# Planning of the counting: 16-bit operands, four buffers, short lists by way of memory, first projections ahead of the picks

## The chip, the core and the metric

The kernel runs on one core of a Trainium2 chip. The metric is the device time of one execution in microseconds. A core has TensorE (matrix products, with a clock that is granted at 1.2 or 2.4 GHz; "cold" and "warm" below), VectorE, ScalarE, GpSimd and SyncE, which here issues the DMAs. Each engine runs its own list of instructions; they meet at semaphores.

## The reference

A chain of four graph networks over 6250 nodes and 100000 edges, sorted by destination. What the step at hand prepares is the first one and the counting of edges for the later ones:

```python
Q = (h @ Wq.T).reshape(N, 8, 16); K = (h @ Wk.T).reshape(N, 8, 16); V = (h @ Wv.T).reshape(N, 8, 16)
score = einsum('ehd,ehd->eh', K[src], Q[dst]) / 4
s = exp(clip(score, -5, 5))[:, :, None]
wV = segment_sum(V[src] * s, dst); z = segment_sum(s, dst)
h_attn = (wV / (z + 1e-6)).reshape(N, 128)
...
agg = segment_sum(x[src], dst)     # in the later networks; here by a matrix of counts
```

## The kernel before, in words

Nodes are handled in 49 blocks of 128 (BLOCKS), in 7 groups (GROUPS) of 7 blocks (GB). Edges lie in tiles of 128; their tile numbers are kept in ROWS = 7 rows of 128 (COLS = 896 in all). For the later networks the kernel builds a matrix of counts in memory (`adjacency`), window by window: a window is 8 destination nodes, and a list of WCOLS = 1664 steps says which edge tile is counted into which window. The function `plan_windows` (L1895 to L2063) makes that list and what goes with it, between the first planning (`plan`) and the attention (`attend`), which starts when all engines have left it.

VectorE in `plan_windows`: after the iota and a memset of the ring of slots by GpSimd (L1943, L1944) and the load of `dst` and `src` (L1914) it casts both (L1960), makes `rank` (L1961 to L1963), copies the ramp four times over as 16-bit numbers (`fours`, L1964), and makes seven masks 1664 wide (L1968). TensorE multiplies each by ones (four products of 416 columns, L2048), which counts how many tiles begin by each step. VectorE reads the sums (`wtile`, L1970) and makes seven masks that pick the tile of each step (L1974). TensorE uses them to draw the rows of `dst` and `src` (eight products for each mask, L2054). Two buffers, `two`, carry the masks, in 32-bit numbers. VectorE makes `window` (L1975), waits for the picks, turns them into `ct.lo` and `ct.place` (L1978 to L1992), and then makes four lists of integers (`ct.tables`, L1996 to L2041), all on whole 128 x 1664 tiles of which it keeps 32 partitions each. `attend` and `score` read one partition of each list into registers.

TensorE's projections (Q, K and V of all blocks, one product of 384 columns for each block, L2062) wait for `taken`, which VectorE raises after it has read the picks (L1980). ScalarE copies each block out of PSUM (L1938, L1939) into `q` and into one of two staging buffers. SyncE loads `xT` for two groups ahead (L1919) and stores each group's K and V to the table in memory (L1928). From the third group on, ScalarE waits for the store of two groups earlier.

## Time and profile before

| | us |
|---|---|
| runs | 5399.48, 5402.13, 5411.69 (median 5402.13) |
| the profiled execution | 5400.67, span 5398.3 |
| `plan` | up to about 38.5 |
| `plan_windows` | 38.5 to 186.0 |
| granted TensorE clock over the span | 0.885 of full |

The page shows TensorE busy for 81% of the whole span, VectorE 66%, GpSimd 51% and ScalarE 42%; these are means over very different steps. For the step at hand one reads the stretches by engine first, and then the order in time of each engine.

### The profile page before, as it was taken

The numbers are of one execution on the slowest core, as the hardware profiler recorded it, in microseconds if no ns is written. First come the engines' busy times: TensorE is split into PE (matmuls) and PEld (weight loads), VectorE is DVE, ScalarE is ACT, GpSimd is POOL, SyncE is SP. The second block draws the span as 40 slices with busy tenths as digits, with TensorE's granted clock in tenths as the row PEclk, the third lists the DMA queues.
The fourth block names the chain that finished last, engine by engine and source line by source line (L and its number), as shares of the span: only waits on it lengthen the run. The fifth ranks groups of instructions, "written<-read, shape, count | busy, mean of one in ns | idle before, by whom it ended". The sixth has DMA issues, their size and how long they took to land. (4 is left out here: it accounts for less than half of the span.)

```text
span 5398.3 us, 99723 instructions
## 1 busy us (share of the span) xinstructions
PE 4350.4 (81%) x24072; PEld 3655.1 (68%) x24073; DVE 3580.8 (66%) x7929; ACT 2266.3 (42%) x4134; POOL 2766.0 (51%) x2730
## 2 busy tenths in 40 slices
PE   7566666766767777777468849999999999999998
PEld 4455555554344444444257639999999999999998
DVE  4888888888778888888776674444445654444444
ACT  0333434343245555555246644444444443344333
POOL 0477777774077777777221104444444443344433
PEclk8788888888977787777789959999999999999999
DMA  1444444443267777777235434343444443233332
GB/s 41 124 117 117 118 117 117 116 118 99 96 182 198 200 200 197 203 201 202 70 111 157 136 114 152 132 154 145 149 155 156 174 141 118 96 144 138 133 126 95
DMA packets 543103, 750.01 MB, mean 139 GB/s; under 512 B 57967, under 2 KB 441966, under 8 KB 542734
## 3 DMA queue, kind: packets, MB, share of 16 engines
q1 hardware_dynamic: 461182, 521.35, 28.8%
q0 software_dynamic: 81552, 224.63, 15.5%
q8 instruction: 123, 2.02, 0.1%
q14 instruction: 246, 2.02, 0.1%
HBM read 584.36 MB, written 161.41 MB: 138 GB/s over the span
## 5 line engine op out<-in xcount | busy, mean ns | idle before, releaser
L544 POOL DMA_INDIRECT arena<-table_kv,arena x1664 | 1721.9, 1035 | 653.5 <-issue 506.4
L2350 PE MATMUL ps<-moving,parts 128*128 128x384 f32 (+1 forms) x11662 | 2015.3, 331 | 36.3 <-ACT moving L2412 20.4
L2350 PEld LDWEIGHTS ps<-moving,parts 128*128 128x128 f32 x11662 | 1948.7, 188 | 70.1 <-ACT moving L2412 29.4
L2291 POOL CAST moving<-counts 128x1152 fp32r<-128x1152 uint8 (+1 forms) x420 | 476.7, 1135 | 736.8 <-PE ps L2350 604.7
L340 ACT ACTIVATE counted<-ps 128x392 uint8<-128x392 f32 x1568 | 665.0, 502 | 324.5 <-PE ps L331 283.7
L2291 POOL CAST moving<-big 128x1152 fp32r<-128x1152 uint8 (+1 forms) x413 | 468.4, 1134 | 608.6 <-PE ps L2350 608.6
L331 PE MATMUL ps<-by_place,by_lo 128*128 128x392 bf16 x1568 | 631.3, 525 | 101.9 <-DVE by_place L295 95.5
L654 PE MATMUL ps<-arena 128*128 128x137 f32 x1664 | 325.2, 352 | 338.1 <-DVE arena L788 322.3
L2412 ACT ACTIVATE moving<-counts 128x1152 fp32r<-128x1152 uint8 (+1 forms) x360 | 366.9, 1024 | 436.5 <-PE ps L2350 433.6
L2412 ACT ACTIVATE moving<-big 128x1152 fp32r<-128x1152 uint8 (+1 forms) x354 | 360.4, 1023 | 429.2 <-PE ps L2350 429.0
L654 PEld LDWEIGHTS ps<-arena 128*128 128x128 f32 x1664 | 276.8, 242 | 367.6 <-ACT arena L699 217.6
L2557 DVE CAST moving<-counts 128x1152 fp32r<-128x1152 uint8 (+1 forms) x240 | 312.8, 1303 | 287.2 <-PE ps L2350 287.2
L2557 DVE CAST moving<-big 128x1152 fp32r<-128x1152 uint8 (+1 forms) x236 | 307.5, 1303 | 288.8 <-PE ps L2350 288.8
L562 PEld LDWEIGHTS ps<-arena 128*128 128x128 bf16 x1680 | 141.6, 123 | 523.5 <-DVE arena L556 450.8
L321 DVE TENSOR_TENSOR slots<-slots,counted 128x196 uint16 x1568 | 406.6, 259 | 89.1 <-DVE slots L321 43.0
L562 PE MATMUL ps<-arena 128*128 128x128 bf16 x1680 | 199.6, 252 | 271.5 <-DVE arena L556 269.0
L295 DVE TENSOR_TENSOR by_place<-count_fours,count_place 128x1568 bf16<-128x1568 f16 (+1 forms) x497 | 395.6, 796 | 0.0
L331 PEld LDWEIGHTS ps<-by_place,by_lo 128*128 128x128 bf16 x1568 | 187.7, 123 | 249.2 <-issue 179.2
L883 PE MATMUL ps<-big,arena 128*128 x1672 | 313.5, 348 | 0.4 <-ACT arena L909 0.4
L883 PEld LDWEIGHTS ps<-big,arena 128*128 128x128 f32 x1672 | 292.3, 257 | 27.9 <-issue 18.6
L666 PE MATMUL ps<-big,arena 128*128 x1680 | 288.9, 330 | 0.4 <-ACT arena L694 0.4
L704 ACT ACTIVATE arena<-arena 128x32 f32<-128x32 f32 x208 | 48.3, 232 | 571.5 <-DVE arena L781 571.5
(329 smaller groups left out, 5311.9 us busy)
## 6 DMA issues: line engine op xcount, KB each, us to landing
counts<-adjacency SPq DMA_DIRECT2D x53, 2352.0 KB, 8.6
big<-adjacency SPq DMA_DIRECT2D x52, 2352.0 KB, 8.5
adjacency<-slots SPq DMA_DIRECT2D x784, 98.0 KB
edge_values<-arena SPq DMA_DIRECT2D x208, 256.0 KB, 3.3
arena<-edge_values SPq DMA_DIRECT2D x208, 256.0 KB, 3.2
arena<-table_kv,arena POOLq DMA_INDIRECT x1664
big<-table_norm SPq DMA_DIRECT2D x60, 192.0 KB, 5.6
big<-adjacency SPq DMA_DIRECT2D x7, 1568.0 KB, 6.5
```

The source lines that it names most:

```text
L295: return dve.tensor_tensor(ct.by_place[:, r % 2, n], ct.fours[:, n], copies(ct.place[:, ds(c * HALF, HALF)], 1, last - first), ALU.is_equal)
L321: dve.tensor_tensor(ct.slot_pairs[:, ds(to[k], WIDE // 2)], ct.slot_pairs[:, ds(of[k], WIDE // 2)], ct.counted_pairs[:, r % 2, k, :], ALU. ...
L331: pe.matmul(m.bank(bank, WIDE), ct.by_lo[:, r % 2, :, k], ct.by_place[:, r % 2, :, k], start=True, stop=True).then_inc(ct.product, 1)
L340: act.activation(ct.counted[:, r % 2, k, :], m.bank(bank, WIDE), ACT.Copy).then_inc(ct.moved, 1)
L544: pool.indirect_dma_start(m.ring4[r][:, k * 2 * D:(k + 1) * 2 * D], None, table, bass.IndirectOffsetOnAxis(m.src[:, j * HALF + k:j * HALF ...
L562: mm = pe.matmul(bank[:, k * P:(k + 1) * P], m.hit16[:, r, :, k], m.ident16, start=True, stop=True)
L654: mm = pe.matmul(summed(k), m.hit[:, r % 2, k, :], m.msg[:, r % 2, k, :], start=True, stop=True)
L883: mm = pe.matmul(m.bank(6 + h)[:, k * P:(k + 1) * P], m.hitT[:, h, k, :], m.q[:, ds(at[k] * D, D)], start=True, stop=True)
L2291: pool.tensor_copy(to, of).then_inc(by_pool, 1)
L2350: mm = pe.matmul(m.bank(g % 2, n * P), d.parts[SOURCE[u]][:, s + q, t_, :], moving[:, q * n * P:(q + 1) * n * P], start=(s + q == 0 and t_ ...
L2412: act.activation(to, of, ACT.Copy).then_inc(by_act, 1)
L2557: dve.tensor_copy(to, of).then_inc(by_dve, 1)
```

## The change

All of it is in `plan_windows`, its buffers and two small tensors in memory.

- The masks are written as bf16, in four buffers instead of two; the ones that they are multiplied with are bf16 too. The rows of `dst` and `src` are split into a bf16 part `high` and the rest `low`, each exact, and each picked product is made twice, once for each part, into the same sum. ScalarE makes `high` and the 32-bit copy; GpSimd makes `low` by a subtraction. GpSimd's memset of the slots comes after that, and VectorE does not wait for it at the start.
- `window` is made ahead of the picks. SyncE writes one partition of it to memory (`windows`) and reads it back as 104 partitions of 16 columns, three times: as it is, shifted by one step, and shifted by two. The four lists are computed on these small tiles while the picks run (38 operations), go to memory (`places`), and from there to one partition each of `ct.tables`.
- The copy into `fours` comes after the masks of the picks.
- TensorE projects group 0 ahead of the counts and group 1 between counts and picks, into PSUM banks 4 to 7; groups 2 to 6 follow the picks as before. The picks wait for `windowed`, `rested` (the subtraction) and the copies of both groups.

The list operations in the middle are left out below; they are those of L2001 to L2041 on the small tiles.

```diff
+FOLD = 16
+FOLDS = WCOLS // FOLD
...
+        self.fold = take(20 * FOLD)
...
+EARLY = 2
...
-        dst_i, src_i = m.rows_i[:, 0:COLS], m.rows_i[:, COLS:2 * COLS]
-        dst_f, src_f = m.rows_f[:, 0:COLS], m.rows_f[:, COLS:2 * COLS]
+        dst_i = m.rows_i[:, 0:COLS]
+        high, low = (w.bitcast(BF16)[:, 0:2 * COLS] for w in m.wints[1:3])
+        ones = m.small[:, 64:64 + P // 2].bitcast(BF16)
         q = WCOLS // 4
-        two = m.wwork[0:2]
...
+        def bank_of(n):
+            return 4 + n % 4 if n < EARLY * GB else n % 8
...
+            def store(g):
                 if g + 2 < GROUPS:
                     load(g + 2)
                 sp.wait_ge(copied, (g + 1) * GB)
                 sp.dma_start(group_rows(table, g), blocks(kv[g % 2], 2 * D)).then_inc(stored[g % 2], 16)
+            load(0)
+            load(1)
+            store(0)
+            sp.wait_ge(windowed, 1)
+            sp.dma_start(windows[0:1, 1:1 + WCOLS], m.window[0:1, :]).then_inc(spread, 16)
+            sp.dma_start(windows[0:1, 0:1], m.window[0:1, WCOLS - 1:WCOLS]).then_inc(spread, 16)
+            sp.dma_start(windows[0:1, 1 + WCOLS:3 + WCOLS], m.window[0:1, WCOLS - 2:WCOLS]).then_inc(spread, 16)
+            sp.wait_ge(spread, 48)
+            for to, first in ((before, 0), (now, 1), (later, 3)):
+                sp.dma_start(to, windows[0:1, first:first + WCOLS].rearrange("o (p c) -> (o p) c", c=FOLD)).then_inc(folded, 16)
+            store(1)
+            sp.wait_ge(tabled, 1)
+            sp.dma_start(places.rearrange("k (p c) -> p k c", c=FOLD), lists.rearrange("p (k c) -> p k c", c=FOLD)).then_inc(placed, 16)
+            sp.wait_ge(placed, 16)
+            for k in range(4):
+                sp.dma_start(ct.tables[32 * k:32 * k + 1, :], places[k:k + 1, :]).then_inc(listed, 16)
+            for g in range(2, GROUPS):
+                store(g)
             for k in range(2):
                 sp.wait_ge(stored[k], 16 * ((GROUPS + 1 - k) // 2))
+            sp.wait_ge(listed, 64)
...
+            act.wait_ge(rows_in, 32)
+            act.activation(high, m.rows_i, ACT.Copy).then_inc(narrow, 1)
+            act.activation(m.rows_f, m.rows_i, ACT.Copy).then_inc(narrow, 1)
...
+                    act.wait_ge(projected, n + 1)
+                    act.activation(m.q[:, n * D:(n + 1) * D], m.bank(bank_of(n))[:, 0:D], ACT.Copy)
...
+            pool.memset(ones, 1.0).then_inc(made, 1)
+            pool.iota(f_ramp, [[1, FOLD]], base=0, channel_multiplier=FOLD).then_inc(made, 1)
+            pool.wait_ge(narrow, 2)
+            pool.tensor_tensor(low, m.rows_f, high, ALU.subtract).then_inc(rested, 1)
             pool.memset(ct.slots[:, :], 0.0).then_inc(made, 1)
...
-            dve.wait_ge(made, 2)
+            dve.wait_ge(made, 3)
             then(dve.tensor_copy(m.wramp, m.wint))
             dve.wait_ge(rows_in, 32)
-            then(dve.tensor_copy(m.rows_f, m.rows_i))
             then(dve.tensor_scalar(first_i, dst_i[:, 0:COLS:P], WIN.bit_length() - 1, None, ALU.arith_shift_right))
             then(dve.tensor_copy(first_f, first_i))
             then(dve.tensor_tensor(rank, first_f, m.tile_id[:, :], ALU.add))
-            then(dve.tensor_copy(ct.fours, copies(m.wramp[:, 0:WIDE], 2, HALF)))
             for j in range(ROWS):
-                if j >= 2:
-                    dve.wait_ge(counted, 4 * (j - 1))
-                dve.tensor_scalar(two[j % 2], m.wramp, rank[:, j:j + 1], None, ALU.is_ge).then_inc(compared, 1)
+                if j >= 4:
+                    dve.wait_ge(counted, 4 * (j - 3))
+                dve.tensor_scalar(two[j % 4], m.wramp, rank[:, j:j + 1], None, ALU.is_ge).then_inc(compared, 1)
             dve.wait_ge(counted, 4 * ROWS)
             then(dve.tensor_scalar(by4(m.wtile), ps4(0), -1.0, 0.0, ALU.add, ALU.max))
+            then(dve.tensor_tensor(m.window, m.wramp, m.wtile, ALU.subtract))
+            dve.sem_inc(windowed, 1)
             for j in range(ROWS):
-                if j >= 2:
-                    dve.wait_ge(drawn, j - 1)
-                dve.tensor_scalar(two[j % 2], m.wtile, m.tile_id[:, j:j + 1], None, ALU.is_equal).then_inc(picked, 1)
-            then(dve.tensor_tensor(m.window, m.wramp, m.wtile, ALU.subtract))
+                if j >= 4:
+                    dve.wait_ge(drawn, j - 3)
+                dve.tensor_scalar(two[j % 4], m.wtile, m.tile_id[:, j:j + 1], None, ALU.is_equal).then_inc(picked, 1)
+            then(dve.tensor_copy(ct.fours, copies(m.wramp[:, 0:WIDE], 2, HALF)))
+            dve.wait_ge(folded, 48)
+            then(dve.tensor_copy(f_int, now))
+            then(dve.tensor_scalar(f_int, f_int, RING - 1, None, ALU.bitwise_and))
+            then(dve.tensor_scalar(to_list, f_int, float(WIDE // 2), None, ALU.mult))
...
+            then(dve.tensor_copy(at_list[:, 0:FOLD:2], f_slot[:, 0:FOLD:2]))
+            then(dve.tensor_copy(at_list[:, 1:FOLD:2], f_block[:, 0:FOLD:2]))
+            dve.sem_inc(tabled, 1)
             dve.wait_ge(drawn, ROWS)
...
-            first, second, third, fourth = (ct.tables[32 * k:32 * (k + 1), :] for k in range(4))
-            then(dve.tensor_copy(i0, m.window))
-            then(dve.tensor_scalar(i0, i0, RING - 1, None, ALU.bitwise_and))
-            then(dve.tensor_scalar(first, i0[0:32, :], float(WIDE // 2), None, ALU.mult))
...
         @block.tensor
         def _(pe):
+            def project(g):
+                pe.wait_ge(loaded[g % 2], 16 * (g // 2) + 16)
+                for b in range(GB):
+                    n = g * GB + b
+                    wait(pe, copied, n - 3 if n < EARLY * GB else n - 7)
+                    pe.matmul(m.bank(bank_of(n), 3 * D), xT[g % 2][:, b * P:(b + 1) * P], m.w["wqkv0"][:, 0, :],
+                              start=True, stop=True).then_inc(projected, 1)
+            project(0)
             for j in range(ROWS):
                 pe.wait_ge(compared, j + 1)
                 for k in range(4):
-                    pe.matmul(m.bank(k, q), m.ones[:, :], two[j % 2][:, k * q:(k + 1) * q],
+                    pe.matmul(m.bank(k, q), ones, two[j % 4][:, k * q:(k + 1) * q],
                               start=(j == 0), stop=(j == ROWS - 1)).then_inc(counted, 1)
+            project(1)
+            pe.wait_ge(windowed, 1)
+            pe.wait_ge(rested, 1)
+            pe.wait_ge(copied, EARLY * GB)
             for j in range(ROWS):
                 pe.wait_ge(picked, j + 1)
                 for k in range(8):
-                    rows = (dst_f, src_f)[k // 4]
-                    mm = pe.matmul(m.bank(k, q), rows[:, j * P:(j + 1) * P], two[j % 2][:, (k % 4) * q:(k % 4 + 1) * q],
-                                   start=(j == 0), stop=(j == ROWS - 1))
+                    at = k // 4 * COLS + j * P
+                    for n, part in enumerate((high, low)):
+                        mm = pe.matmul(m.bank(k, q), part[:, at:at + P], two[j % 4][:, (k % 4) * q:(k % 4 + 1) * q],
+                                       start=(j == 0 and n == 0), stop=(j == ROWS - 1 and n == 1))
                 mm.then_inc(drawn, 1)
             pe.wait_ge(taken, 1)
-            for g in range(GROUPS):
-                pe.wait_ge(loaded[g % 2], 16 * (g // 2) + 16)
-                for b in range(GB):
-                    wait(pe, copied, (g - 1) * GB + b + 1)
-                    pe.matmul(m.bank(b, 3 * D), xT[g % 2][:, b * P:(b + 1) * P], m.w["wqkv0"][:, 0, :],
-                              start=True, stop=True).then_inc(projected, 1)
+            for g in range(EARLY, GROUPS):
+                project(g)
...
+    windows = nc.dram_tensor("windows", (1, WCOLS + 3), F32, kind="Internal").ap()
+    places = nc.dram_tensor("places", (4, WCOLS), I32, kind="Internal").ap()
...
```

## Rows read from the trace of the kernel before

**Rows 1.** Busy time by stretch: from:to, length, each engine's busy time (instructions), clock, DMA
```profile
38.50:186.00 147.50, 97.94 (x266) 53.01 (x266) 86.20 (x73) 25.39 (x99) 7.43 (x2) 0.82 0.23 72
```
**Rows 2.** Order in time, VectorE: start, duration, engine, line, operation, idle before
```profile
46.17 1.03 DVE L1958 CAST big<-arena 128x1664 f32<-128x1664 int32 x1 [8.79 <-POOL slots L1944]
...
48.56 0.17 DVE L1962 CAST small<-small 128x7 f32<-128x7 int32 x1
...
73.98 1.89 DVE L1970 TENSOR_SCALAR big<-ps 128x1664 f32<-128x1664 f32 x1 [4.50 <-PE ps L2048]
75.91 1.09 DVE L1974 TENSOR_SCALAR big<-big,tile_id 128x1664 f32<-128x1664 f32 x1
76.91 1.08 DVE L1974 TENSOR_SCALAR arena<-big,tile_id 128x1664 f32<-128x1664 f32 x1
...
118.23 1.89 DVE L1978 SCALAR_TENSOR_TENSOR big<-big,ps 128x1664 f32<-128x1664 f32 x1 [8.36 <-PE ps L2054]
...
134.34 1.03 DVE L1996 CAST arena<-big 128x1664 int32<-128x1664 f32 x1
...
186.00 0.07 DVE L729 MEMSET arena<- 128x8 f32 x1 [1.65 <-PEq L366]
```
**Rows 3.** Order in time, TensorE
```profile
51.12 5.92 PE L2048 MATMUL ps<-big,ones 128*128 128x416 f32 x8 [16.64 <-DVE big L1968]
...
77.05 7.55 PE L2054 MATMUL ps<-big,arena 128*128 128x416 f32 x16 [3.10 <-DVE big L1974]
...
122.16 15.45 PE L2062 MATMUL ps<-w,arena 128*128 128x384 f32 x42 [4.04 <-DVEq L1980]
```
**Rows 4.** Stretches as in group 1: the third us of the picks
```profile
79.00:80.00 1.00, 1.00 (x2) 0.36 (x2) 0.00 (x0) 0.00 (x0) 0.00 (x0) 0.50 0.00 0
```
**Rows 5.** DMA issues with KB and time to landing; then min/median/max of the table stores
```profile
arena<-in_xT SPq DMA_DIRECT2D x2, 448.0 KB, 6.0
...
arena<-in_src SPq DMA_DIRECT2D x1, 448.0 KB, 5.2
...
DMA to landing us min/median/max: 4.0/5.8/6.8
```
**Rows 6.** ScalarE and SyncE in order of time, and a cast's group from the page
```profile
39.12 0.56 SPq L1914 DMA_DIRECT2D arena<-in_src  x1
...
147.66 0.52 ACT L1939 ACTIVATE arena<-ps 128x256 f32<-128x256 f32 x1
...
148.21 9.78 SPq L1928 DMA_DIRECT2D table_kv<-arena  x3
...
L2412 ACT ACTIVATE moving<-counts 128x1152 fp32r<-128x1152 uint8 (+1 forms) x360 | 366.9, 1024 | 436.5 <-PE ps L2350 433.6
```
**Rows 7.** Line L1099, the nearest 16-bit products: ns min/median/max; then order in time
```profile
L1099 PE MATMUL ps<-arena x448: 166/270/539, 2742.9 to 3107.6; 128*128 128x396 bf16 x75, 128*128 128x4 bf16 x75
...
2900.21 0.21 PEld L1099 LDWEIGHTS ps<-arena 128*128 128x128 bf16 x2
2900.32 0.34 PE L1099 MATMUL ps<-arena 128*128 128x396 bf16 x2
```
**Rows 8.** GpSimd in order of time, and VectorE beside it in two places
```profile
40.16 5.98 POOL L1944 MEMSET slots<- 128x7056 uint8 x1
...
2753.52 2.09 POOL L1074 TENSOR_TENSOR arena<-arena 128x896 f32<-128x896 f32 x1
2753.52 2.63 DVE L1170 TENSOR_TENSOR arena<-arena,big 128x512 f32<-128x512 f32 x1 [0.22 <-PE ps L1112]
...
3219.00 2.24 POOL L2291 CAST moving<-counts 128x1152 fp32r<-128x1152 uint8 x2 [128.99 <-DVE counts L2425]
3220.24 1.21 DVE L2432 TENSOR_SCALAR dense_cut<-big 128x384 int32<-128x384 int32 x1
...
3222.15 0.36 DVE L2432 TENSOR_SCALAR dense_cut<-big 128x384 int32<-128x384 int32 x1
```
**Rows 9.** DMA issues of the whole span: the adjacency stores
```profile
adjacency<-slots SPq DMA_DIRECT2D x784, 98.0 KB
```

More of the change, by code:

```diff
@@ L76 @@
 assert WSTEPS + 2 < WCOLS and WCOLS % 4 == 0 and WCOLS // 4 <= 512 and SLOTS % 2 == 0
+FOLD = 16
+FOLDS = WCOLS // FOLD
+assert WCOLS == FOLD * FOLDS and FOLDS <= P and FOLD % 2 == 0
 RING = 16
@@ new lines, in _ @@
+            then(dve.tensor_copy(ct.fours, copies(m.wramp[:, 0:WIDE], 2, HALF)))
[3 more added lines that the diff above has]
+            then(dve.tensor_scalar(to_list, f_int, float(WIDE // 2), None, ALU.mult))
+            then(dve.tensor_tensor(same, now, before, ALU.is_equal))
+            then(dve.tensor_copy(f_real, f_int))
+            then(dve.scalar_tensor_tensor(f_real, f_real, -float(RING), same, ALU.add, ALU.mult))
@@ new lines, in _ @@
+            then(dve.tensor_scalar(of_list, f_real, float(RING), float(WIDE // 2), ALU.add, ALU.mult))
+            then(dve.tensor_copy(f_int, now))
+            then(dve.tensor_scalar(f_int, f_int, 1, None, ALU.arith_shift_right))
+            then(dve.tensor_copy(f_even, f_int))
+            then(dve.tensor_copy(f_int, later))
+            then(dve.tensor_scalar(f_int, f_int, 1, None, ALU.arith_shift_right))
+            then(dve.tensor_copy(f_step, f_int))
+            then(dve.tensor_tensor(f_step, f_step, f_even, ALU.subtract))
@@ L2003, in _ @@
-            then(dve.tensor_copy(b, i0))
-            then(dve.scalar_tensor_tensor(b, b, -float(RING), a, ALU.add, ALU.mult))
-            then(dve.tensor_scalar(second, b[32:64, :], float(RING), float(WIDE // 2), ALU.add, ALU.mult))
-            even, real = m.wtile, b
-            then(dve.tensor_copy(m.wint, m.window))
-            then(dve.tensor_scalar(m.wint, m.wint, 1, None, ALU.arith_shift_right))
-            then(dve.tensor_copy(even, m.wint))
-            then(dve.memset(c, 0.0))
-            then(dve.tensor_tensor(c[:, 0:WCOLS - 2], even[:, 2:WCOLS], even[:, 0:WCOLS - 2], ALU.subtract))
```

72 lines of the change are left out of this document (33 added, 39 removed).

## Prediction

> **What bounds the kernel now.** I read the table of stretches first. The change touches only the step between 38.5 and 186.0 us, so its ceiling is a part of 147.5 us out of 5398. No engine fills that step [rows 1]. The chain of waits is printed mainly for the end of the program, where TensorE rules, so here I followed the order in time engine by engine. On VectorE [rows 2] the step has four pieces. From 46.17 to 73.98 it makes seven masks for the counts and mostly waits. From 73.98 to 118.23 it makes seven picks, again waiting. From 118.23 to 134.34 it turns the picked rows into slots (16.1 us). From 134.34 it makes four lists without a pause, until the next step starts at 186.00. The idle time printed there is 1.65 us, so the lists end at 184.35: 50.0 us. TensorE [rows 3] shows why VectorE waits in the first two pieces: the products of the picks start at 77.05, and VectorE's idle time before 118.23 is released by the last of them. Its projections begin only at 122.16, and ScalarE empties the seventh block of the fifth group at 148.18 [rows 6]; all of this is hidden under the lists. So the end is set by counts, picks, slots and lists, in series, with projections as second: the last store is issued just before 158.0 [rows 6] and needs 4.0 us at least [rows 5], so they are done by about 162.
>
> **The sum's base.** The profiled execution took 5400.67 us with a span of 5398.3; the median of the three runs is 5402.13, 1.5 above. I subtract in the first and add 1.5 at the end.
>
> **Start, loads and casts.** VectorE no longer waits for the memset of the slots, which ends at 46.14 [rows 8]; it waits for the iota (done by 40.16) and two tiny GpSimd operations. Next it waits for the edge rows: the second load is issued at 39.12 [rows 6] and needs 5.2 us [rows 5], so 44.3. The cast of both rows and the copy into fours leave this place; three short operations stay, 0.17 long [rows 2], which I count at 0.20 with their waits: 44.9. Masks follow each 1.0 apart (75.91, 76.91); I take no less for 16-bit results, since the operand that they read stays 32 bits wide; three are made by 47.9. On ScalarE the two new casts are 1792 wide; 1152 wide take 1.02 [rows 6], so 1.6 each: 47.5.
>
> **First projections ahead.** TensorE had been idle; xT is issued next, at 39.7, and lands 6.0 later [rows 5]: 45.7. A 416-wide 4-byte instruction costs 0.70 cold (5.92 for eight) [rows 3]; a block is two of 384 columns: 1.29 cold. Warm, 112 such instructions take 41.2 us (77.05 to 118.23), of which the first 16 take 7.55: 0.35 each for the others, and a block 0.65. I take four cold and three warm, 7.1 us: 52.8. This is a cost on the path: the first masks are ready from 45.9 on and wait for it.
>
> **Counts.** Two instructions per product were two passes each (416 columns at 2.4 GHz are 0.173 us, and one takes 0.35); with 16-bit operands one pass is left. The nearest 16-bit row, 396 columns, is one of a pair that lasts 0.34, of which the second, 4 columns, is 0.17: so 0.17 from start to start [rows 7]. At 0.175, a count is 0.7 instead of 2.8. Four buffers let VectorE run ahead.
>
> **Who holds the port.** GpSimd's new subtraction is 1792 wide; 896 wide take 2.1 us, so 4.2. Where VectorE ran beside such work, an operation of 512 columns took 2.63 us (1664 columns cost 1.93), and a one-input operation took 1.21 instead of 0.36; each ended shortly after GpSimd's [rows 8]. So from 47.9 to 52.1 the fourth mask waits, and is ready at 53.1; that still costs nothing (TensorE needs it at 54.9). Then GpSimd's memset of 5.98 us follows, now in the middle of the step. No row shows a memset against a VectorE operation: the cost of that lies between 0 and all of it. I take all: the fifth mask is asked for at 53.6 and starts at 59.1. It is ready at 60.1, the others at 61.1 and 62.1. TensorE idles from 55.6 to 60.1 and goes cold, as it does after a 3.1 us pause now (granted 0.50 at 79 us [rows 4]): three counts at 1.4 give 64.2.
>
> The Trainium skill (SBUF — State Buffer, "Who interferes with whom") says that a VectorE operation in a two-port mode and a GpSimd instruction shut each other out for the whole instruction. The two stretched operations agree with it; on memset it would say the same.
>
> **Picks.** The tile and window operations take 1.93 each: 68.1. The first pick is there at 69.1. Meanwhile TensorE projects group 1: 1.3 + 6 × 0.65 = 5.2, until 69.4, and ScalarE's last copy is done at 70.0. The picks are 7 × 8 × 2 = 112 passes at 0.175 = 19.6 (before: 118.23 − 77.05 = 41.2): end at 89.8, with 0.2 for the last one's tail. VectorE's masks (1.0 each 2.8 us) lie under it.
>
> **Lists.** On 104 partitions of 16 columns I count 38 operations. At the 0.20 of the 7-wide ones they are 7.6 us instead of 50.0. They wait for two rounds of three DMAs through memory. I issue each in 0.5 us and let it land in 4.0 to 6.8 (the range of the table stores [rows 5], far larger transfers): from 68.1 that is 79.1 to 84.7. VectorE gets to them at 80.4, after its last mask (79.4, released by the third pick) and the copy into fours. So they end at 88.0, at worst 92.3, against 89.8: I put 0 on the path; with the cover gone 2.5 us. Queued behind this wait is VectorE's wait for the picks. SyncE waits in turn for the lists, for one DMA and four issues, till 97.3 at most; behind it stands the store of group 2, not ready before 89.8 + 3.9 + 7 × 0.65 = 98.3. Nothing.
>
> **After the picks.** Picks done to TensorE's restart stays 122.16 − 118.23 = 3.93. Five groups are left, which in time answer to the first five of before (two start without waiting for a store): 148.18 − 122.16 = 26.0. The last store needs 4.0 once no load runs beside it, and the change of step 1.65. In sum 35.6 us after the picks' end, against 186.00 − 118.23 = 67.8. VectorE needs only 16.1 of it. The projections are the new end of the step.
>
> **Sum.** The next step starts at 89.8 + 35.6 = 125.4 instead of 186.0: 60.6 us less, 5340 for the profiled execution and 5341 with the offset. The steps behind it are unchanged.
>
> **Rivals.**
> 1. The memset doesn't block VectorE. Then masks 5 to 7 are ready at 54.8, 55.8 and 56.8, the counts end warm at 57.8, group 1's copies at 63.0, the picks at 82.8: 7.0 less, 5334. For it: a memset reads nothing, and both rows of blocking are of GpSimd operations that read. Against: these operations write too.
> 2. The weight load isn't hidden under a pass of 0.175 us. It takes 0.1 (0.21 for two) [rows 7]; 112 picks and 12 late counts add 12 us: 5353. Against it: in the 16-bit row the second load (the pair starts at 2900.21) runs while the first product does, and the next starts on time. The Trainium skill (TensorE: Matmul & The Clock Gate, "The mechanism") has loads overlap only where row groups differ. All these have the same row group, so by that rule the load would show; the trace speaks against it.
> 3. The lists come late through memory: 92.3 for 89.8 delays all behind the picks, since VectorE must make the lists before it reads the picks. With transfers as slow as 8 us it is 5 us: 5346.
> 4. Slower than before: the two new tensors in memory stand ahead of the adjacency one and shift it. It takes 784 stores [rows 9] in the long steps that follow, beside gathers whose landing VectorE waits for. To lose more than 60.6 + 10.8, each would have to cost 0.091 us of path; at 0.1 it is 5420. Nothing in the profile asks for it: pieces are small and unaligned already.
> 5. The change moves nothing: the lead of 60 us is lost in the long loop that follows. That needs a clock it keeps time with, and none is seen: 5402.
>
> **How the numbers follow.** Forecast 0.50; rival 1 0.26; rival 2 0.09; rival 3 0.07; rival 4 0.04; rival 5 0.04. The likeliest gives 5341. Forecast and rivals 1 to 3 lie between 5334 and 5353; with 5 us below and 3 above for the bounds of cold blocks, landings and casts, the range is 5329 to 5356. About 0.2% (10.8 us) can be told from no change: faster 0.92, same 0.04, slower 0.04.
>
> **What would show it.** In the changed profile: first attention mask of VectorE near 125; a mask stretched to some 5 us beside the memset, or not (rival 1); a pick group of 16 products starting each 2.8 us (4.4 if rival 2); 38 list operations over before the last pick; TensorE granted 0.50 after a pause in the counts; and SyncE's last wait on a table store. A start of attention above 140, or a longer span behind it, makes me wrong.

## The result and the profile after

The changed kernel takes 5360.22 us, median of 4 runs (5352.53 to 5366.35), beside 5406.91 (5399.48 to 5413.43) for the kernel before on the same chip: a ratio of 0.9913, 95% interval 0.9901 to 0.9926. That is 46.7 us less; 60.6 were forecast, and the time lies 4 us above the range. The profiled execution took 5363.49 us with a span of 5361.2. One execution of the kernel before, beside e17 and e18, took 6401.22 us at a granted clock of 0.613, where the others had 0.88; it is left out below.

First the step itself, as in [rows 1 to 3]. The stretches of the kernel after (length, busy time of TensorE, its weight loads, VectorE, ScalarE and GpSimd with their instructions, granted clock, DMA):

```profile
46.00:69.00 23.00, 18.62 (x56) 9.70 (x56) 20.31 (x11) 9.04 (x28) 10.17 (x2) 0.75 0.20 67
69.00:94.00 25.00, 20.22 (x114) 10.89 (x112) 18.48 (x48) 0.86 (x4) 0.00 (x0) 1.00 0.21 59
94.00:126.00 32.00, 24.95 (x70) 13.77 (x70) 11.84 (x9) 17.43 (x70) 0.00 (x0) 0.89 0.59 187
```

Counts, picks and projections now follow each other with TensorE at work in all three. VectorE in order of time (start, duration, engine, line, operation, idle before):

```profile
45.92 0.17 DVE L2007 TENSOR_TENSOR small<-small,tile_id 128x7 f32<-128x7 f32 x1
46.12 2.08 DVE L2011 TENSOR_SCALAR big<-big,small 128x1664 bf16<-128x1664 f32 x2
48.12 11.32 DVE L2011 TENSOR_SCALAR arena<-big,small 128x1664 bf16<-128x1664 f32 x2
59.36 2.06 DVE L2011 TENSOR_SCALAR big<-big,small 128x1664 bf16<-128x1664 f32 x2
...
68.86 2.08 DVE L2019 TENSOR_SCALAR big<-big,tile_id 128x1664 bf16<-128x1664 f32 x2
...
80.86 0.17 DVE L2023 CAST arena<-arena 104x16 int32<-104x16 f32 x1
...
88.59 0.17 DVE L2060 COPY arena<-arena 104x8 int32<-104x8 int32 x1
90.11 1.89 DVE L2064 SCALAR_TENSOR_TENSOR big<-big,ps 128x1664 f32<-128x1664 f32 x1 [1.34 <-PE ps L2103]
...
126.05 0.07 DVE L733 MEMSET arena<- 128x8 f32 x1 [19.86 <-PEq L370]
```

The last line answers to the last of [rows 2]: attention begins at 126.05 instead of 186.00. The lists take from 80.86 to 88.76, under the picks; where 1.65 us of idle time stood before attention, VectorE now waits 19.86. TensorE and GpSimd:

```profile
46.17 7.00 PE L2085 MATMUL ps<-w,arena 128*128 128x384 f32 x14 [11.48 <-DMA arena<-in_xT]
...
59.50 1.57 PE L2092 MATMUL ps<-arena,small 128*128 128x416 bf16 x4 [4.21 <-DVE arena L2011]
...
70.22 5.79 PE L2103 MATMUL ps<-big,arena 128*128 128x416 bf16 x32 [0.85 <-ACT arena L1980]
75.84 5.79 PE L2103 MATMUL ps<-arena 128*128 128x416 bf16 x32
...
94.03 15.60 PE L2085 MATMUL ps<-w,arena 128*128 128x384 f32 x42 [3.96 <-DVEq L2066]
```

```profile
48.38 4.26 POOL L1988 TENSOR_TENSOR arena<-arena 128x1792 bf16<-128x1792 f32 x1 [7.26 <-ACT arena L1973]
52.58 5.98 POOL L1989 MEMSET slots<- 128x7056 uint8 x1
```

So the step gave 59.95 us. `plan` ahead of it, which nobody edited, ends a little earlier or later in each trace: the load of `src` is issued at 39.12 before and 39.78 after, and between 37.0 and 41.1 over all traces without a hold. Below, "from the load" is the time from that issue to the start of attention, which leaves this out: 146.88 us before, 86.26 after, so 60.6 less. The span shrank by only 37.1, from 5398.3 to 5361.2. To find the rest I took, in every trace, the first and last operation of each stage. From here on four stages count: `attend`, `score`, `sum_values` and the dense part.

| stage, length in us | before | after |
|---|---|---|
| `attend` | 1122.1 | 1124.6 |
| `score` | 1132.5 | 1146.3 |
| `sum_values` | 365.6 | 370.4 |
| dense part | 2180.6 | 2183.2 |

23 of the 60 us came back in these two traces, most of them in `score`, a loop whose code the change doesn't touch. The stretches of `score`, the kernel before, then after (columns as above):

```profile
1486.00:2618.00 1132.00, 800.49 (x3660) 477.49 (x3657) 929.41 (x2348) 597.11 (x1362) 863.93 (x832) 0.77 0.71 197
```
```profile
1428.00:2574.00 1146.00, 807.07 (x3661) 485.48 (x3659) 929.05 (x2349) 596.98 (x1362) 878.05 (x832) 0.76 0.70 195
```

VectorE and ScalarE have the same work within 0.4 us. GpSimd, with the same 832 gathers, is busy 14.1 us longer, which is the whole difference; the stage less GpSimd's busy time is 268 us in both. Its groups in the same two stretches (count, busy us, mean ns, idle before):

```profile
L544 POOL DMA_INDIRECT arena<-table_kv,arena x832 | 864.5, 1039 | 259.8 <-issue 253.2 <-POOLq L366 6.6
```
```profile
L548 POOL DMA_INDIRECT arena<-table_kv,arena x832 | 878.4, 1056 | 259.9 <-issue 252.7 <-POOLq L370 6.6 <-SPq L862 0.6
```

The gathers follow each other 0.30 us apart and never wait for a buffer: GpSimd paces this stage, and also `attend` (832 gathers, none over 0.35 us apart in either trace). What makes a gather longer stands in the order of time. GpSimd, and VectorE beside it, in the kernel after:

```profile
1479.55 0.94 POOL L548 DMA_INDIRECT arena<-table_kv,arena  x1 [0.30 <-issue]
1480.80 2.38 POOL L548 DMA_INDIRECT arena<-table_kv,arena  x1 [0.30 <-issue]
1483.49 0.95 POOL L548 DMA_INDIRECT arena<-table_kv,arena  x1 [0.31 <-issue]
...
1487.25 1.52 POOL L548 DMA_INDIRECT arena<-table_kv,arena  x1 [0.30 <-issue]
```
```profile
1479.80 0.67 DVE L970 TENSOR_REDUCE big<-arena 128x16 f32<-128x512 f32 x1
1480.39 0.41 DVE L293 TENSOR_TENSOR by_lo<-count_fours,count_lo 128x512 bf16<-128x512 f16 x1
1480.72 0.25 DVE L325 TENSOR_TENSOR slots<-slots,counted 128x196 uint16 x1
1480.89 0.97 DVE L299 TENSOR_TENSOR by_place<-count_fours,count_place 128x1568 bf16<-128x1568 f16 x1
1481.78 0.25 DVE L325 TENSOR_TENSOR slots<-slots,counted 128x196 uint16 x1
1481.95 0.42 DVE L560 TENSOR_TENSOR arena<-count_fours,arena 128x512 bf16<-128x512 f16 x1
...
1486.97 0.97 DVE L299 TENSOR_TENSOR by_place<-count_fours,count_place 128x1568 bf16<-128x1568 f16 x1
```

The gather at 1487.25 starts when the comparison (L299) has 0.69 us left, and takes 0.58 longer than 0.94. The one at 1480.80 starts within L325, finds the comparison behind it, and gets through only after L560. I matched every gather of `score` in the kernel before with the VectorE operation that runs as it starts:

| running at its start | time left, us | gather, mean us |
|---|---|---|
| nothing, or L962 (one operand in PSUM), or L966 (reduction) | any | 0.95 |
| the comparison, L295 | 0.3 | 1.11 |
| the same | 0.5 | 1.33 |
| the same | 0.7 | 1.50 |
| the same | 0.9 | 1.78 |

The Trainium skill (SBUF — State Buffer, "Who interferes with whom") says that a VectorE instruction with two inputs in SBUF contends with a GpSimd instruction that reads SBUF, and that one with at most one such input doesn't, outside VectorE's two-port modes. In `score` the trace agrees: only the operations with two such inputs cost a gather anything (0.95 us beside L962 and L966, 1.31 in the mean beside L295). Added up, the gathers that start within the comparison cost 57.8 us over 0.945 each in the kernel before and 71.1 after.

### The profile page after: what moved, and what is told of

It is laid out like the page before. It is cut to its first block and busy times, and to the rows that moved or that the text cites. A ratio compares the mean times of both kernels' runs of the same rounds, so it can differ in the third digit from the quotient of the medians.

```text
span 5361.2 us, 99690 instructions
## 1 busy us (share of the span) xinstructions
PE 4333.2 (81%) x24044; PEld 3651.3 (68%) x24045; DVE 3546.1 (66%) x7926; ACT 2271.4 (42%) x4136; POOL 2789.6 (52%) x2733
## 5 line engine op out<-in xcount | busy, mean ns | idle before, releaser
L2457 ACT ACTIVATE moving<-counts 128x1152 fp32r<-128x1152 uint8 (+1 forms) x360 | 366.9, 1024 | 435.4 <-PE ps L2395 432.6
L325 DVE TENSOR_TENSOR slots<-slots,counted 128x196 uint16 x1568 | 405.6, 259 | 92.6 <-DVE slots L325 43.4
L299 DVE TENSOR_TENSOR by_place<-count_fours,count_place 128x1568 bf16<-128x1568 f16 (+1 forms) x497 | 395.0, 795 | 0.0
L887 PE MATMUL ps<-big,arena 128*128 x1672 | 320.7, 353 | 0.4 <-ACT arena L913 0.4
L670 PE MATMUL ps<-big,arena 128*128 x1680 | 293.4, 333 | 0.4 <-ACT arena L698 0.4
L708 ACT ACTIVATE arena<-arena 128x32 f32<-128x32 f32 x208 | 48.3, 232 | 571.6 <-DVE arena L785 571.6
```

The costliest lines, as they stand in the source:

```text
L299: return dve.tensor_tensor(ct.by_place[:, r % 2, n], ct.fours[:, n], copies(ct.place[:, ds(c * HALF, HALF)], 1, last - first), ALU.is_equal)
L325: dve.tensor_tensor(ct.slot_pairs[:, ds(to[k], WIDE // 2)], ct.slot_pairs[:, ds(of[k], WIDE // 2)], ct.counted_pairs[:, r % 2, k, :], ALU. ...
L887: mm = pe.matmul(m.bank(6 + h)[:, k * P:(k + 1) * P], m.hitT[:, h, k, :], m.q[:, ds(at[k] * D, D)], start=True, stop=True)
L2457: act.activation(to, of, ACT.Copy).then_inc(by_act, 1)
```

## The experiments

Times are medians beside the kernel before on the same chip, run at the same time: 5397.66 for e1 to e4, 5398.38 for e5 to e8, 5404.32 for e9 to e12, 5397.06 for e13 to e16, 5400.31 for e17 and e18.

**Code loading and the place of the tensors (e1 to e4).** In `score` the kernel after loads 9 blocks of code on queue 8 in each turn of the loop, the kernel before none, and TensorE stands 3.8 to 4.6 us at each turn. That, and the two new tensors ahead of the adjacency one (rival 4), were the first suspects. e1 fixes the head of TensorE's loop at slot 0 of a code block, e2 and e3 at slot 224:

```diff
-            with engine.Fori(0, SC_PAIRS) as i:
+            slots = {'PE': 0}
+            at = {engine.engine: slots[str(engine.engine).split('.')[-1]]} if str(engine.engine).split('.')[-1] in slots else None
+            with nc.Fori(0, SC_PAIRS, engines=OrderedEngineSet([engine.engine]), head_slot=at) as i:
```

> The changed kernel with one addition: the first instruction of TensorE's loop in `score` is put at the start of a block of its code (slot 0), whatever stands ahead. Theory (the code theory): the step of the change gained its 60 us, and what was given back is mainly TensorE's loop in `score`, whose code no longer stays loaded because the 56 instructions fewer ahead of it moved its head; the trace shows 9 code packets of 16 KB for each turn, and 4 us of TensorE's idle time at each turn. It expects about 0 packets on that queue for each turn, no such idle time, a turn of 171 us instead of 173, `score` of 1133 us instead of 1146, and a time 10 us below the changed kernel: near 5349. Rival (placement in memory): the two new tensors moved the adjacency tensor; then nothing changes here: 5360. Rival (no cause, only spread): 5360 too.

> The changed kernel with the head of the same loop pinned near the end of a code block (slot 224). Code theory: as the changed kernel, 9 packets for each turn, 5360. Placement and spread: 5360 as well. It shows that pinning itself costs or brings nothing.

> The kernel before with the head of TensorE's loop in `score` pinned at slot 224. Code theory: it takes the loss that the change took: packets go from 0 to 9 for each turn, `score` gets 10 to 13 us longer, time near 5417. Placement and spread: as before, 5407.

 (e3 is the kernel before with the same edit.)

e4 declares `windows` and `places` behind `adj`:

> The changed kernel with its two new tensors declared behind the adjacency tensor, which so lies where it lay before. Placement theory: the 13 us that were given back come again, 5347. Code theory and spread: no difference, 5360.

Measured: e1 5350.58 (−47.1), e2 5343.11 (−54.6), e3 5396.69 (−1.0), e4 5351.15 (−46.5). The traces are sharper than the times. Code loads in one turn of `score`, e1 (queue, kind: packets, MB, share), then e3:

```profile
q14 instruction: 26, 0.21, 0.4%
```
```profile
q14 instruction: 28, 0.23, 0.4%
q8 instruction: 9, 0.15, 0.4%
```

e1 has no loads on queue 8, and its `score` is still 1145.3 us. e3 has them in each turn, and its `score` is 1131.8. Nor do the loads make the pause of TensorE at the turn. Its longest pause there is 5.1 to 5.5 us in the kernel before and 5.0 to 5.3 in e1, against 3.8 to 4.6 after and 4.1 to 5.1 in e3; all its idle time within 9 us of the turn is 6.5 to 7.3, 7.1 to 7.5, 6.8 to 8.9 and 6.2 to 7.2. VectorE stands 3.3 to 4.9 us at its own turn in all four, and without the loads TensorE waits for it. TensorE in the kernels before, e1 and after, and VectorE before, each at one turn:

```profile
1761.09 0.62 PE L562 MATMUL ps<-arena 128*128 128x128 bf16 x4 [5.46 <-DVE arena L556]
```
```profile
1879.26 0.62 PE L567 MATMUL ps<-arena 128*128 128x128 bf16 x4 [5.15 <-DVE arena L561]
```
```profile
1871.19 1.56 PE L335 MATMUL ps<-by_place,by_lo 128*128 128x392 bf16 x4 [3.83 <-issue]
```
```profile
1759.05 0.43 DVE L289 TENSOR_TENSOR by_lo<-count_fours,count_lo 128x512 bf16<-128x512 f16 x1 [3.99 <-issue]
```

GpSimd gathers through all of it, 0.30 us from one gather to the next, so these pauses are off the path. This theory fell, and so did rival 4. e2, with the loads, came out 7 us better than the changed kernel, where no difference was expected; its trace has a `score` of 1135.7 and a `sum_values` of 362.8, and nothing here says why.

**Chance, memset, position, and half of the comparison (e5 to e8).** e5 is the changed kernel again. e6 moves one line:

```diff
+            pool.memset(ct.slots[:, :], 0.0).then_inc(made, 1)
             pool.wait_ge(narrow, 2)
             pool.tensor_tensor(low, m.rows_f, high, ALU.subtract).then_inc(rested, 1)
-            pool.memset(ct.slots[:, :], 0.0).then_inc(made, 1)
```

> The changed kernel as it is, a second time, as the measure for its neighbours. Seen so far: in `score` the 832 gathers of GpSimd run back to back, 0.30 us apart; the length of `score` less GpSimd's busy time in it is the same in six traces (268.2 to 269.1 us), and the busy time alone differs: 863.9 and 862.9 us in two traces of the kernel before (with and without a moved loop head), 878.1, 877.0, 866.6 and 869.5 us in four of the changed kernel. A gather takes 0.94 us alone and up to 2.4 us when VectorE's comparison of count_place (0.97 us) begins late in it. Theory A (the loss is in the gathers, by where the comparisons fall in them, and the changed kernel tends to the longer side): median 5345 to 5355, `score` 1138 to 1147 us. Theory B (chance alone; the gain is the step's 60 us on average, and the runs so far were unlucky): median 5335 to 5342, `score` about 1132 us.

> The 5.98 us memset of the slots moved on GpSimd ahead of its wait for the 16-bit halves, so that it runs during the loads and no longer beside VectorE's third and fourth mask. Those two masks took 11.32 us together, the two before them 2.08 us each. Theory: they take 4.2 us together, the window and all behind it come 6 to 7 us earlier, attention's first VectorE operation is at 119 to 120 us instead of 126.1, and the median is 6 to 7 us under that of the changed kernel beside it. Rival: the masks then collide with GpSimd's subtraction (4.26 us) instead, or the picks wait for the low halves: attention starts at 124 to 126 and nothing is gained. Second rival: attention starts at 119 to 120, but the time is lost in the gathers of the two long loops (spread between runs of one kernel: some 10 us).

e7 (`HOLD` = 75) puts this stage between `plan` and `plan_windows`:

```diff
+    with Phase(nc, "hd", "held") as (block, held):
+        @block.scalar
+        def _(act):
+            for k in range(HOLD):
+                wait(act, held, k)
+                act.activation(m.wwork[0][:, 0:512].rearrange("p (n q) -> p n q", n=4), copies(m.ones[:, :], 1, 4), ACT.Copy).then_inc(held, 1)
```

> The changed kernel with a hold between `plan` and `plan_windows`: 75 copies on ScalarE, one after another (0.6 us each and the wait between them, some 60 us in all); everything behind it happens later by the hold, nothing else differs. Theory C (the loss hangs on when attention begins, so that what the step gains is partly given back by position in time): `score` falls back to about 1132 us, and the time is that of e5 plus the hold less some 10 us. Theory D (it does not): the median is that of e5 plus the hold, within 3 us, and `score` and `sum_values` stay as long as in e5.

e8 computes half of the columns of a comparison:

```diff
-                    count_place(dve, ct, c + 1, p + 1).then_inc(ct.hot, 1)
+                    count_place(dve, ct, c + 1, p + 1, 0, WIDE // 2).then_inc(ct.hot, 1)
```

> Left out: the upper half of the columns of VectorE's comparison of count_place in the loop of `score` (784 elements of 1568, about 0.49 us instead of 0.97, 170 times; half of the counting there is not computed anew). Theory A (`score` is paced by GpSimd's gathers, and what lengthens them is mostly this comparison beside them): a gather's mean in `score` falls from about 1.05 to 1.00 us or less and `score` from 1132 to 1147 us down to 1085 to 1115 us, and `score` less GpSimd's busy time stays at 268 to 269 us. Rival E (`score` is paced by VectorE's own chain of counting): it falls by most of the time taken off VectorE, 75 to 85 us, to 1050 to 1070 us, with waits of GpSimd for free buffers as before. Rival F (by TensorE or by the transfers): it changes by less than 5 us.

Measured: e5 5353.46 (−44.9), so the loss is no bad luck of a few runs. e6 5344.42 (−54.0), 9.0 below e5. e7 5401.76, that is e5 + 48.3 for a hold that moved attention by 50.5 us (125.6 to 176.1): by the times theory D holds within its 3 us, and the position in time is worth little. Its other half, that `score` stays as in e5, did not hold in the traces: 1136.6 us in e7 and 1149.7 in e5, whose traced execution (5365.68) was 12 us longer than its other three. VectorE in e6, in order of time:

```profile
38.34 6.76 DVE L2003 CAST big<-arena 128x1664 f32<-128x1664 int32 x1 [3.56 <-POOL arena L1986]
...
45.74 5.39 DVE L2011 TENSOR_SCALAR big<-big,small 128x1664 bf16<-128x1664 f32 x2
51.05 2.07 DVE L2011 TENSOR_SCALAR arena<-big,small 128x1664 bf16<-128x1664 f32 x2
...
119.11 0.07 DVE L733 MEMSET arena<- 128x8 f32 x1 [20.74 <-PEq L370]
```

and the first ScalarE operation that waits for the same load of `src`:

```profile
42.30 1.70 ACT L1972 ACTIVATE arena<-arena 128x1792 bf16<-128x1792 int32 x1 [4.48 <-DMA arena<-in_src]
```

The memset now stretches a cast (6.76 us instead of 1.03), and the masks lose only the subtraction's time: from the first to the end of the seventh they take 10.4 us, 16.3 in the kernel after, so a memset beside them costs 5.9. But the stretched cast ends at 45.10, when the rows have been there since 42.3, so that the masks begin some 2.4 us later after their load than they did. Net, attention starts 82.15 us from the load, against 85.80 in e5 and 85.0 to 86.8 in the eight traces with the later memset (80.6 to 82.4 in the five with the early one): the moved line gives about 4 us. The rest of the way from 125.6 to 119.1 is `plan`, which ended 2.8 us earlier in this trace, and 5 of the 9.0 us in the medians are not the step's.

e8's own time (13346.17 us) says nothing: with half of the counting left out, the kernel's flag sends it down its second, much longer path afterwards. Its `score` does tell. The stretch and GpSimd's group in it:

```profile
1420.00:2524.00 1104.00, 791.29 (x3657) 474.55 (x3656) 831.98 (x2350) 590.18 (x1349) 836.31 (x834) 0.79 0.73 203
```
```profile
L548 POOL DMA_INDIRECT arena<-table_kv,arena x832 | 835.2, 1004 | 259.9 <-issue 250.0 <-POOLq L370 6.6 <-SPq L862 3.4
```

VectorE was relieved of 97 us (929 to 832). `score` fell by the 43 to 46 us by which the gathers fell (878 and 882 in after and e5, 836 here), to 1103.6. A stage paced by VectorE would have given most of the 97. Theory A holds: the gathers set the pace, and VectorE's comparison sets part of their length. (The expectation's 170 comparisons were a miscount: there are 286.)

**Edits elsewhere, and one part undone (e9 to e12).** e9 is e7's hold in the kernel before. e10 sets VectorE's loop head to slot 0 as e1 did TensorE's. e11 is e6 and e2 together.

> The kernel before with the same hold as e7 (75 copies on ScalarE between `plan` and `plan_windows`; it delayed attention by 50.5 us there). Theory G (the kernel before happens to have its comparisons well placed against the gathers, and any edit ahead of the loops loses some of that): the time is the kernel before plus 50.5 us plus 5 to 12 us, `score` 1137 to 1147 us, and the same for `sum_values` (370 us instead of 364 to 366). Theory H (what the changed kernel loses comes from its own edits): the kernel before plus 50.5 us within 3 us, `score` 1130 to 1134 us.

> The changed kernel with the head of VectorE's loop in `score` put at the start of a code block (TensorE's was moved in e1 and e2, VectorE's never). Theory I (the place of VectorE's code sets how the comparisons fall in the gathers): `score` comes to 1130 to 1134 us and the time falls by 8 to 12 us against e5. Rival (it sets no more than TensorE's did): `score` stays between 1134 and 1149 us, the time within 4 us of e5's 5353.

> e6's early memset together with e2's head of TensorE's loop at slot 224; each alone gave a median below that of the changed kernel (5344.4 and 5343.1 against 5350 to 5353). If both last: 5335 to 5338, attention from 118 to 119 us, `sum_values` 363 us as in e2 (370 to 371 in the six other traces of the changed kernel). If e2's was chance: 5342 to 5346 and `sum_values` 370 us.

e12 projects nothing early; both early calls of `project` and of `store` go behind the picks and the lists:

```diff
-EARLY = 2
+EARLY = 0
```

> One part undone: no group of the projections ahead of the picks, all seven behind them as in the kernel before (28 projections more there, at 0.375 us each by the 70 that run there now: 10.5 us); the rest is as changed. Forecast's view (the first projections run in time that TensorE would wait): attention starts 9 to 11 us later than 126, at 135 to 137, and the time is 9 to 11 us longer. Rival (ScalarE's copies or the transfers of the lists end the step, and the early projections are worth little): it starts at 127 to 131.

Measured: e9 5461.90 (+57.6; attention at 235.4, so the hold is 49.4 and 8.2 are extra, or 6 when `plan`, 2 us shorter in this trace, is counted out), `score` 1139.4 but `sum_values` 359.4: half as theory G has it (370 was expected for `sum_values`). e10 5356.13 (−48.2), `score` 1148.8: VectorE's code isn't it. e11 5341.63 (−62.7; interval of the ratio 0.9860 to 0.9893), attention at 119.65, `sum_values` 366.9: between its two expectations. e12 5366.07 (−38.3), where it was expected:

```profile
136.81 0.07 DVE L733 MEMSET arena<- 128x8 f32 x1 [29.88 <-PEq L370]
```

Attention starts 98.97 us from the load, 12.7 later than in the kernel after (by the clock 136.81 against 126.05, since `plan` was 1.9 us shorter). The early projections are worth these 12.7 us of the 60, a little more than the 9 to 11 expected.

**Cutting the long operations (e13 to e18).** If what is left of an operation is what a gather waits for, two short ones in its place should cost less. e13 and e14 stand on e6, e15 and e17 on the kernel before:

```diff
-                    count_place(dve, ct, c + 1, p + 1).then_inc(ct.hot, 1)
+                    count_place(dve, ct, c + 1, p + 1, 0, WIDE // 2)
+                    count_place(dve, ct, c + 1, p + 1, WIDE // 2, WIDE).then_inc(ct.hot, 1)
```

> e6 (memset early) with VectorE's comparison of count_place in the loop of `score` cut into two operations of 784 elements (0.56 us each, e8; before 0.97 for both), nothing left out. Theory A (a gather waits for the rest of the comparison that runs when it starts): in e6's `score` the gathers that start within it cost 59 us over 0.94 us each; cut in two the rest is half as long, so that 25 to 35 us of them go; GpSimd's busy time in `score` 867 to 835 to 845 us, `score` 1102 to 1115 us, the time 20 to 30 us below e6. Rival J (a gather gets no turn between two VectorE operations that follow at once; some gathers of 2.2 to 2.4 us waited through three of them): the gathers stay as long and `score` changes by less than 5 us, or grows. Rival K (VectorE becomes the bound by its 43 us more work): `score` above 1150 us, with GpSimd waiting for buffers.

e14, e17 and e18 also cut attention's product of the messages, in two (e18: in four):

```diff
+                for part in (slice(0, HALF // 2), slice(HALF // 2, HALF)):
+                    op = dve.tensor_tensor(m.msg[:, h, part, 0:D].rearrange("p k (n c) -> p k n c", c=C0),
+                                           rows[:, part, D:2 * D].rearrange("p k (n c) -> p k n c", c=C0),
+                                           copies(m.msg[:, h, part, D:D + H0], 3, C0), ALU.mult)
+                op.then_inc(weighted, 1)
```

> e13 with attention's product of the messages (128x512 f32 of two operands in SBUF, 0.686 us x208) cut in two as well. In e6's `attend` the 181 gathers that start within it cost 57.8 us over 0.94 us each. Theory A: some 20 to 30 us of that go, `attend` 1095 to 1105 us instead of 1125, while the product from PSUM of the same size costs them nothing (0.3 us or less for all) and is left whole. Rival K: VectorE, busy 972 of 1125 us there, takes some 20 us more and its chain (multiplied, reduced, weights, messages) sets the time: `attend` 1120 us or longer.

> The kernel before with the comparison of `score` cut in two as in e13. Theory A: the gathers within the comparison cost 57.8 us there, so it gains 20 to 30 us as well, and `score` ends within 5 us of e13's (what made the two kernels differ in `score` is mostly gone). Rival J, K: as for e13.

> The kernel before with a hold of one copy instead of 75 (it adds a stage of 1 to 3 us ahead of `plan_windows`, and nothing behind it is edited). Theory G (any edit ahead moves the comparisons off a lucky place): the time is the kernel before plus 5 to 12 us, `score` 1137 us or more. Theory H: the kernel before plus 1 to 3 us, `score` 1130 to 1134 us, and e9's 7 us more than its hold come from elsewhere.

> The kernel before with both cuts of e14. Attention falls from 1122 to about 1099 us as it did in e14 (1125 to 1101) and `score` to about 1123 as in e15: the time is 22 to 26 us below e15's 5389.6, at 5363 to 5368. Against e14 (5305.0, with attention's start at 122.3 instead of about 184.5): the difference is 58 to 63 us if the step's 62 us now last but for the few us of `sum_values` (366 against 370 us); under 52 us if something else in the long loops still takes them.

> e14 with attention's product of the messages in four operations of 128x128 instead of two of 128x256 (0.379 us each). By the law seen so far (a gather waits for the rest of the operation that runs when it starts) the waits halve again: another 8 to 12 us off `attend` (1101 us), time 5293 to 5299. Rival (VectorE's added work, some 0.07 us for each piece and 30 us in all, takes over; its busy time in `attend` was 982 of 1101 us): `attend` stays at 1098 to 1104 or grows.

| | time, against before | `attend` | `score` | `sum_values` |
|---|---|---|---|---|
| e6 | 5344.42, −54.0 | 1124.7 | 1134.4 | 370.3 |
| e13 | 5332.20, −64.9 | 1123.7 | 1129.3 | 373.7 |
| e14 | 5304.96, −92.1 | 1101.0 | 1122.5 | 370.3 |
| e18 | 5308.52, −91.8 | 1104.1 | 1122.8 | 371.0 |
| e15 | 5389.59, −7.5 | 1122.1 | 1123.1 | 366.9 |
| e17 | 5364.02, −36.3 | 1100.6 | 1122.0 | 366.6 |
| e16 | 5411.69, +14.6 | 1121.0 | 1136.7 | 361.9 |

`attend` and `score` of e14 (stretches, columns as above):

```profile
122.00:1223.00 1101.00, 774.08 (x4600) 644.69 (x4600) 981.74 (x2817) 441.92 (x1043) 835.91 (x832) 0.84 0.41 118
1401.00:2523.00 1122.00, 807.54 (x3659) 485.73 (x3657) 947.80 (x2634) 594.61 (x1362) 853.59 (x832) 0.76 0.72 199
```

The cut of the messages does what was expected: VectorE gets 10 us more work in `attend`, GpSimd 24 less (860 to 836), and the stage is 24 us shorter. The cut of the comparison does less than half of what I expected (25 to 35 us in e13): gathers of 1.5 us and more fall from 41 to 6, but those that start within a comparison still cost 52.4 us instead of 59.2. The second piece starts as soon as the first ends, and many gathers seem to get no turn between the two; that is argued from the sizes and wasn't tested by itself. In e14, with the same code in `score`, they cost 44.0, so some 8 us of such a sum come and go with the places. In e18 the gathers shrink by another 3 us (836 to 833 in `attend`), yet the stage grows by 3: it runs on for 17.6 us after the last gather, where e14 took 11.6. VectorE, now busy 992 us instead of 982, seems to be what is late, as the rival of e18 had it. The best version is e14: 5304.96 us (5303.01 to 5309.66), ratio 0.9826 to the kernel before, interval 0.9812 to 0.9839.

e17 answers what is left. With the same cuts in both kernels `attend` and `score` differ by 0.4 and 0.5 us (1101.0 and 1100.6, 1122.5 and 1122.0), though 13.8 us lay between the `score` of the first two traces. Of the 61.7 us between the starts of attention (183.9 and 122.2) the times keep 55.8, each taken against the kernel before beside it (the two traced spans differ by 54.1). That lies between the two forecasts of e17, 58 to 63 and under 52. What is still lost is 3.7 us in `sum_values`, a stage of TensorE, and 1.5 in the dense part.

## Why the prediction was wrong, step by step

- **Start and masks.** The masks started at 46.12 (44.9 forecast; 0.66 of it is `plan`) and the fifth at 59.36 (59.1). The memset does block a VectorE operation with one input: two masks took 11.32 us instead of 2.08. One of them alone took 10.33, through the subtraction and the memset both, where the forecast let the fourth mask in between them; the end is the same. Rival 1 fell. Its price, 7.0 us for a memset that blocks nothing, no run shows; e6 shows 5.9 in the masks and about 4 net. Of the two stretched operations of [rows 8], only L2432 has one input as the masks have; L1170 has two inputs in SBUF, and the prediction took both as the same case.
- **Counts.** TensorE went cold as forecast (four products in 1.57 us at 59.50); counts over at about 64.9 (64.2).
- **Picks.** 32 products take 5.62 us from start to start, so a group of 16 takes 2.81 (2.8 forecast) and no weight load shows: rival 2 fell. The picks end at 90.1 (89.8).
- **Lists.** 38 operations of 0.21 us from 80.86 to 88.76 (88.0 forecast): 0 on the path, with 1.3 us to spare. Rival 3 fell.
- **After the picks.** TensorE restarts 3.96 us after them (3.93), attention starts at 126.05 (125.4). The forecast of the step was off by 0.65 us in 60.6, and that is the 0.66 by which `plan` ended later; such closeness is partly luck: counted out of that, the masks started 0.6 late, counts and picks were 0.9 shorter than forecast and the tail 0.3 longer.
- **"The steps behind it are unchanged."** This is the term that failed. It was taken as 0 and measured 23 us in the profiled pair, 13 to 15 in the medians of the changed kernel (46.7 and, in e5, 44.9 us gained of 60). In its place the runs showed a `score` that is longer by what its gathers are longer: 14.1 us in the pair. Rival 5 had the loss, at the wrong size and with the wrong condition. I asked for a clock that the loop keeps time with. What it has is a stage paced by gathers, whose length hangs on where VectorE's two-input operations fall in them. The row for that was in the profile (one group of 1664 gathers with a mean of 1.035 us, though most take 0.94), and I had not looked at what set it. [Rows 8] had the mechanism too, used only inside the step. Rival 4, and with it a change of the transfers, fell with e4.
- **What differs in detail.** In ten traces with the changed step and a whole comparison (after, e1, e2, e4 to e7, e10 to e12) `score` lasts 1134.4 to 1149.4 us, mean 1142; in the kernel before and e3 1132.5 and 1131.8. Not all of this comes with the edit. A traced execution is one of 4 to 12, and its `score` goes with where it stands among them: 1134 to 1144 us where the traced time lay at or below the median of its own kernel (e2, e4, e6, e7, e12), 1143 to 1149 where it lay 3 to 12 us above (after, e1, e5, e10, e11). So `score` seems to move by some 10 us from one execution to the next of the same kernel, and single traces can't rank edits more finely than that; the medians carry the 13 to 15 us. Shown is how the stage gets longer: in all of these the stage follows GpSimd's busy time, e8 and e14 shorten both by acting on VectorE alone, and with the cuts the difference is gone (e17). Not settled is why the kernel before has the better places. It isn't TensorE's or VectorE's loop head (e1 to e3, e10), the tensors (e4) or the time at which attention begins (e7, by its median). A stage of one copy ahead of the step cost the kernel before 14.6 us in the median (e16; 6 to 23 by the interval, its own length of 2.5 included) and one of 75 some 8 beyond its length (e9), so its places can be lost by edits that touch neither loop; but the traced executions of e16 and e9 were among their fastest and show only 4 to 7 us of it, and e3's edit cost nothing. Which instruction ahead decides I can't say.
- **`sum_values`** has 370 to 371 us in most traces with the changed step (362.5 in e2, 366.9 in e11, 373.7 in e13), 359 to 367 in the others. TensorE paces it; its granted clock there is 0.92 to 0.94 in the long ones and 0.925 to 0.95 in the short ones. What moves the clock wasn't tested.
- **The range.** Its upper end (5356) came from rivals inside the step. A stage of 1100 us with 832 gathers of scattered length, twice, deserved 10 to 15 us of its own.

## What to carry to other kernels

- When a step is shortened, read what paces the long stages behind it: if that is an engine whose instructions have scattered lengths (here gathers, 0.94 to 2.4 us), treat such a stage as able to give or take 1% of its length, though nothing in it is edited, and read such differences from medians of several executions, not from one trace.
- Beside a GpSimd that gathers without a pause, the length of one VectorE operation with two inputs in SBUF matters more than the sum of its work: two of 256 columns for one of 512 gave 24 us of 1125, for 10 us more VectorE work. It isn't a rule: two of 784 for one of 1568 gave 5 to 10 of 1133, and four products of 128 in place of the two of 256 gave nothing.
- Put a long GpSimd memset where VectorE has nothing to do until after its end. In the middle of a chain of masks 5.98 us of it cost 5.9; moved to the loads it still reached 2.4 us past them, because VectorE had a cast there.
- Compare a step by its length from its own first instruction: `plan`, unedited, moved the start by up to 4 us.

## What the runs showed of the hardware

- A gather of 128 rows on GpSimd takes 0.94 us and 0.30 to the next. Starting while VectorE compares two operands in SBUF it takes about 0.94 plus what is left of that operation less 0.1; starting within an operation with an operand in PSUM, or a reduction, of the same 0.68 us it takes 0.95.
- A GpSimd memset of 5.98 us shuts out VectorE operations with one input: two masks (f32 to bf16) took 11.32 us beside it and the subtraction instead of 2.08, a cast (int32 to f32) 6.76 instead of 1.03.
- Nine code blocks loaded in every turn of TensorE's loop, or none, by the place of the loop's head alone (e1, e3), made no difference to a stage that GpSimd paced; TensorE's longest pause in a turn was 3.8 to 5.1 us with the loads and 5.0 to 5.5 without.
- 16-bit products of 416 columns, each with a 128x128 weight load of its own, follow each other every 0.176 us (5.62 us for 32).
